# Attention heads of a fused four-layer kernel: more keys and values formed ahead, first expert rows fetched one stage earlier, deltas split in two parts

## The reference, cut to what matters

```
x = x + cross_attention0(layernorm(x), context)     # 16 heads of 16, softmax over 64 context rows
x = x + mixture0(layernorm(x))                      # 8 experts, top 2, then a layer norm of its own
x = x + cross_attention1(layernorm(x), context)
x = x + quantum_ffn(layernorm(x))
x = x + window_attention(context, layernorm(x))
x = x + mixture2(layernorm(x))                      # 8 experts, top 2, exact gelu
x = x + cross_attention3(layernorm(x), context)
x = x + ternary_ffn(layernorm(x))
```

## Time and profile before

| | us |
|---|---|
| median of three runs | 2132.32 |
| lowest and highest run | 2128.41 and 2132.96 |
| the profiled execution, its own time | 2133.32 |
| its span in the profile | 2131.5 |
| granted PE clock, mean | 0.945 of full |

### The profile page before, as it was taken

The page is one execution under the profiler, slowest core; times in us unless marked ns, Lnnn a source line. Parts: engine busy times, 40 slices in busy tenths (PEclk is TensorE's granted clock), DMA queues, the critical chain, the costliest instruction groups (busy, mean ns, idle before and its releaser), DMA issues. The chain is left out here.

```text
span 2131.5 us, 37545 instructions
## 1 busy us (share of the span) xinstructions
PE 1908.1 (90%) x11960; PEld 1414.1 (66%) x11961; DVE 1253.5 (59%) x2609; ACT 951.4 (45%) x2160; POOL 624.9 (29%) x716
## 2 busy tenths in 40 slices
PE   6999499999849996999999579999999995999787
PEld 3666356666526663666676379999999993666455
DVE  5787656666467876888655622222222214998886
ACT  2555434444346643333234333333333333555787
POOL 2223346656446721011001222222222222332000
PEclk9999699999969998999989589999999997999999
DMA  8000211121171004000001511111111114100001
GB/s 289 11 21 31 107 50 63 61 64 59 52 234 61 2 1 173 1 0 0 0 24 47 208 50 39 35 34 39 34 37 37 34 32 170 41 21 1 16 24 40
DMA packets 71619, 119.69 MB, mean 56 GB/s; under 512 B 13920, under 2 KB 55264, under 8 KB 68448
## 3 DMA queue, kind: packets, MB, share of 16 engines
q1 hardware_dynamic: 56304, 79.02, 10.6%
q0 software_dynamic: 13632, 37.24, 5.6%
q10 hardware_dynamic: 1584, 2.13, 0.3%
HBM read 87.03 MB, written 31.33 MB: 56 GB/s over the span
## 5 line engine op out<-in xcount | busy, mean ns | idle before, releaser
L1586 ACT ACTIVATE e_hT<-psum,x_bt 128x128 f32<-128x128 f32 x568 | 154.7, 383 | 340.4 <-PE psum L1549 340.4
L1549 PEld LDWEIGHTS psum<-e_xT,e_w 128*128 128x128 f32 x2272 | 266.4, 193 | 7.2 <-ACT e_xT L1579 3.6
L1549 PE MATMUL psum<-e_xT,e_w 128*128 128x128 f32 x2272 | 267.1, 276 | 3.0 <-ACT e_xT L1579 3.0
L1558 PE MATMUL psum<-m_w,e_hT 128*128 x1136 | 256.8, 379 | 0.0
L1558 PEld LDWEIGHTS psum<-m_w,e_hT 128*128 128x128 f32 x1136 | 210.4, 190 | 25.7
L1608 DVE COPY e_w<-m_w 128x2048 f32 x71 | 87.1, 1227 | 223.9 <-PE psum L1549 222.5
L1405 ACT ACTIVATE e_hT<-psum,x_bt,x_gt 128x128 f32<-128x128 f32 x284 | 107.0, 457 | 143.5 <-PE psum L1372 143.5
L1490 POOL DMA_INDIRECT rows_out<-e_y,dst x106 | 105.6, 996 | 207.0 <-DVE e_y L1618 175.1
L883 DVE TENSOR_REDUCE a_mx<-psum 128x16 f32<-128x1024 f32 x96 | 116.6, 1215 | 73.3 <-PE psum L631 73.1
L1482 POOL DMA_INDIRECT e_x<-rows_in,src x142 | 142.3, 1002 | 56.6 <-issue 35.3
L774 ACT ACTIVATE a_pT<-psum 128x512 f32<-128x512 f32 x192 | 103.9, 594 | 116.2 <-PE psum L687 116.1
(11 more groups left out here) (333 smaller groups left out, 3537.5 us busy)
## 6 DMA issues: line engine op xcount, KB each, us to landing
m_w<-in_L_ffn_w SPq DMA_DIRECT2D x16, 1024.0 KB, 12.1
m_w<-in_L_ffn_w SPq DMA_DIRECT2D x16, 512.0 KB, 11.1
m_w<-rows_out SPq DMA_DIRECT2D x16, 512.0 KB, 5.9
a_ar_g<-rows_out SPq DMA_DIRECT2D x16, 512.0 KB, 4.9
rows_in<-a_r_z SPq DMA_DIRECT2D x14, 512.0 KB, 2.9
x_res<-in_x SPq DMA_DIRECT2D x8, 512.0 KB, 7.4
m_w<-rows_in SPq DMA_DIRECT2D x8, 512.0 KB, 3.9
out_x<-x_res SPq DMA_DIRECT2D x8, 512.0 KB, 2.9
```

The source lines that it names most:

```text
L1549: mm = pe.matmul(h_b[s][:, f, :], w1[:, kk, f * P:(f + 1) * P], xT[s][:, kk, :], start=(kk == 0), stop=(kk == DC - 1))
L1558: mm = pe.matmul(y_b[s][:, 0:D], hT[s][:, f, :], k.w2[:, bass.ds(e * (FC * D) + f * D, D)], start=(f == 0), stop=(f == FC - 1))
L1586: g = act.activation(hT[s][:, f, :], h_b[s][:, f, :], ACT.Gelu, bias=bt[:, bass.ds(e * FC + f, 1)])
```

## The change

It has four parts. `held` is the number of batches whose keys and values are held at once, and `HEAD[L]` says how many of them PE forms at each of four places ahead of the loop.

1. **Keys and values ahead.** Layers 0 and 1 hold three batches: one is formed ahead of the turns, two after scores(0). Layer 3 holds all eight: four ahead of the turns, one after the turns, one after the queries, two after scores(0). Ahead of the loop they go into four banks that are otherwise unused there (`val_b`, `sum_b`, `out_b`, `pr_b`), one batch a bank in layers 0 and 1, two in layer 3, and are counted by a semaphore of their own, `kv_ps`. DVE drains a batch when all that shares its bank has been formed (`kv_formed`). In the loop step b forms batch b + held.
2. **Two banks for the first turns and queries.** For b = 0, c = 1 the turn and the queries use the bank `sc_b[1]`. Neither turn waits for a drain, and the queries wait for both turns' drains alone. On ACT `normalise(1)` moves behind the drains of the first queries (layers 0 and 3; in layer 1 it was there).
3. **First rows in the experts' stage.** SP itself waits for the scatters at the end of the stage, then issues the transfers of batch 0 (three in m0, two in m2), in `first_rows`. Their buffers, the experts' weights and the raw ternary weights are now parts of one tensor `m_wide`.
4. **Deltas in two parts.** `split_delta` runs for the 64 columns of batch 0 ahead of the first drain of keys, and for the other 448 where it stood.

The lines that carry it, cut:

```
+HEAD = {0: (1, 0, 0, 2), 1: (1, 0, 0, 2), 3: (4, 1, 1, 2)}
...
-        kb = [sb(f"{nm}kb{s}", [P, DC * GW]) for s in range(2)]
+        kb = [sb(f"{nm}kb{s}", [P, DC * GW]) for s in range(held)]
-        va = [sb(f"{nm}va{s}", [P, H // 2, 2, DK]) for s in range(2)]
+        va = [sb(f"{nm}va{s}", [P, H // 2, 2, DK]) for s in range(held)]
...
+        kv_banks = [val_b, sum_b, out_b, pr_b]
+        per = -(-held // len(kv_banks))
+        def kv_formed(b):
+            return min(held, (b // per + 1) * per) if b < held else b + 1
+        def front(b, c):
+            return sc_b[1] if b == 0 and c == 1 else pr_b
...
             def _(pool):
-                for s in range(2):
+                for s in range(held):
                     pool.memset(va[s][:, :, :, :], 0.0).then_inc(va_zero, 1)
...
                 def turn(b, c):
                     if c == 0:
                         pe.wait_ge(z_done, b + 1)
-                        pe.wait_ge(k_done, b + 1)
-                        pe.wait_ge(v_done, b + 1)
-                    else:
+                        if b:
+                            pe.wait_ge(k_done, min(NB, b - 1 + held))
+                            pe.wait_ge(v_done, min(NB, b - 1 + held))
+                    elif b:
                         pe.wait_ge(drained, DRAINS * b + 1)
...
                 def queries(b, c):
-                    pe.wait_ge(drained, DRAINS * b + 2 + c)
+                    pe.wait_ge(drained, DRAINS * b + 2 + (c if b else 0))
...
-                        if t == 3 and b + 2 < NB:
-                            keys_values(b + 2)
+                        if t == 3 and b + held < NB:
+                            keys_values(b + held)
...
-                keys_values(0)
+                after = [sum(formed[:i]) for i in range(len(formed) + 1)]
+                for b in range(after[0], after[1]):
+                    keys_values(b)
                 for c in range(DC):
                     turn(0, c)
+                for b in range(after[1], after[2]):
+                    keys_values(b)
                 for c in range(DC):
                     queries(0, c)
+                for b in range(after[2], after[3]):
+                    keys_values(b)
                 pe.wait_ge(drained, DRAINS)
                 pe.wait_ge(k_done, 1)
                 scores(0, 0, 0)
-                keys_values(1)
+                for b in range(after[3], after[4]):
+                    keys_values(b)
...
                 if loading:
-                    act.wait_ge(split, 7 + DSPLIT - 1)
+                    act.wait_ge(split, SPLITS)
...
-                drain_keys(0, 0)
-                drain_values(0, 0)
+                first = 3 if arrival else 1
+                if loading:
+                    split_delta(0, slice(0, S))
+                for b in range(first):
+                    drain_keys(b)
+                    drain_values(b)
...
                 if loading:
                     statistics(1)
-                    split_delta()
+                    split_delta(1, slice(S, NB * S))
                 if arrival:
                     arrival.add(dve, 1)
                     arrival.statistics(dve, 1)
+                early = held - formed[3]
+                for b in range(first, early):
+                    drain_keys(b)
+                    if b < held - 1:
+                        drain_values(b)
                 softmax(0, 0)
-                drain_keys(1, 1)
+                for b in range(early, held):
+                    drain_keys(b)
+                    if b < held - 1:
+                        drain_values(b)
...
             def _(sp):
                 if k.next_att is not None:
                     load_attention(sp, k, k.next_att)
+                    first_rows(sp, k, L)
...
+def first_rows(sp, k, L):
+    rows_sent(sp, k)
+    u, y = sum_buffers(k) if L == 0 else (None, got_buffers(k))
+    if L == 0:
+        sp.dma_start(u[0], normed_rows(k, 0)).then_inc(k.first_in[L], 16)
+    for j in range(TOPK):
+        sp.dma_start(y[j][0], expert_rows(k, j, 0)).then_inc(k.first_in[L], 16)
```

151 lines of the change are left out of this document (93 added, 58 removed).

## The result

| | before | after |
|---|---|---|
| median, us | 2131.02 (4 runs) | 2112.19 (4 runs) |
| lowest and highest | 2128.41, 2132.96 | 2107.66, 2114.22 |
| the profiled execution, its own time | 2133.32 | 2110.33 |
| its span | 2131.5 | 2108.5 |
| granted PE clock, mean | 0.945 | 0.948 |

The ratio is 0.9909, with a 95% interval of 0.9897 to 0.9921: 18.8 us less by the medians. The forecast was 2114.0, its range 2104 to 2124.

What follows compares the result with a forecast made beforehand. It took PE to bound the attention loops, with idle waits and low clock in the heads. Layers 0, 1 and 3 gave -7.6 - 4.7 - 7.0 = -19.3 us from 2133.3: forecast 2114, range 2104 to 2124.

Steps and rivals of the forecast that it cites:

- DVE is just in time: Layer 0's head: the second part of the split ends at 25.7, so the softmax starts at 26.7, not 32.97.
- rival (5): Softmax(0) held by the split's second part in layer 0, by drains 4 and 5 in layer 3; about 2130; chance 0.04.
- The barriers come 1.4 us later: End of m0 before layer 1: SP's 1.4 us of issue delays the barriers, to 589.4.
- they landed at 602.02 ... I take 599: Layer 1's head: batch 1's rows land at 599, between 597.3 and 602, so z comes 3.0 us earlier.
- low all through: Two banks for first turns and queries: worth 1.65 us a layer, with PE's clock low throughout.
- a case of -4.5 and one of -12.5: Layer 3: -4.5 if the four batches run at the low clock, -12.5 if it rises during them; -7 taken.
- 6.4 for both queries (the clock rising within them): Layer 3's head: both queries take 6.4 us, after 3.0 for the fifth batch; scores at 1795.7, 2.0 later than before.
- issue nothing: Costs put at nothing: `kv_ps` and the one tensor for weights and buffers add no instructions.
- (1): Layer 3's crowded head eats its gain; third context landing at 1779 makes it +1.5, total 2122.5; chance 0.13.
- (2): Clock rises in layer 3's four batches (-12.5) and layer 0's head is at its fast end (-9): 2107; chance 0.12.
- (3): The early fetch brings nothing: layer 1 becomes -0.5, layer 3 about -6, total 2119; chance 0.06.
- (4): Slower: clock stays at 1.2 GHz after PE's waits; decides at 45 us more low stretches, 2140 with 60; chance 0.03.

Runs made afterwards that it cites:

- the tensor alone: The kernel before, with only the experts' weights and raw ternary weights made parts of one tensor m_wide: 2127.39 us, ratio 0.9991.
- the first run: The changed kernel with batch 0's rows fetched in the attention stage again, not in the experts' stages: 2118.12 us, ratio 0.9936 to the kernel before.
- the contexts' experiment: The changed kernel, layer 3 issuing contexts of batches 0 to 3 before batch 1's rows, PE awaiting POOL's zeroes only before its scores: 2110.13 us, ratio 0.9898.
- the unused products: The changed kernel with 16 extra 128x512 products on PE in layer 1 ahead of the turns, their results unused: 2113.04 us, ratio 0.9904.

## Why the prediction was right

The median came out 1.8 us under the forecast, and the forecast's case held: the heads of all three attentions got shorter at the places named, and the loops by the batches that left them. Its terms were less good than its sum, and that the sum came so near is in part luck. By the two profiles the attentions gave 6.4 us more than forecast; 2.6 us that the rest took back, and 4.2 by which the two profiled executions lie further apart than the medians, made up for it. Undoing them one by one bears out parts 2, 3 and 4. For part 1 no run shows a gain that is clear of the spread: it shortens the loops, and the heads take all or much of it back.

**Layer 0**, -7.6 against -9.0 in the profile. Right: the turns start at 15.43 (forecast 15.25), nine passes over 64 columns took 2.3 us (2), the loop gives 1.6. The queries ran at the high clock, 3.70 us, where 6.3 were forecast, so the scores began at 22.66 and not at 25.3. Of these 2.6 us only 1.2 reached the softmax (25.54, forecast 26.7): "DVE is just in time" failed, since its second part of the split ended at 25.5 and the scores had been there since 23.9. This is rival (5) in small. From that softmax to the scores of tile 2 it took 7.7 us, forecast 7.9. The high clock of the queries was a matter of the execution: of the eight profiles with this code in layer 0 four have them at 3.70 us and four at 5.7 to 6.3, near the forecast, and the stage took 214.3 us on average in both groups. The mean is -8.2 against the profile before and -6.2 against that of the tensor alone; the term of -7.6 lies between.

**Layer 1**, -4.7 against -7.2. Three steps failed. "The barriers come 1.4 us later": they did not move. And "they landed at 602.02 ... I take 599": the rows of batch 1 were there 15.9 us after the last scatter, where 599 means 17.1. So z came 4.1 us earlier and not 3.0. From z to the first scores 3.3 us went instead of 1.65: the banks gave 1.5, and the clock, "low all through" in the forecast, rose within the queries (6.05 us, not 7.5). The third batch cost 1.6 behind the scores (1.5 forecast), and the loop gave 1.4 (1.6).

**Layer 3**, -7.0 against -9.5. The forecast had a case of -4.5 and one of -12.5, by the clock, and took a value between. The four batches did run at the low clock, as its slow case says, and held the turns, 3.2 us behind z. But then the clock rose: from the turns to the first scores it took 8.4 us, where the slow case has 13.6 (1782.1 to 1795.7). So the scores came 4.5 us earlier and not 2.0 later. The step that failed is "6.4 for both queries (the clock rising within them)", with the fifth batch at 3.0: they took 3.70 and 1.6. From the scores to those of tile 2 it was 3.4 us more than before (3.15 forecast), and the loop gave 8.4 and not 9.7: a batch whose keys and values leave this loop makes it 1.42 us shorter (22.36 to 20.94), where the term took the 1.62 that lie between their start and that of the next work. The same code gave 198.9, 199.0, 199.0, 200.3 and 202.6 us in five executions, that is -5.9 to -9.6. Between the ends of the forecast it is the clock that chooses, from one execution to the next.

**The rest.** The forecast put `kv_ps` and the one tensor at nothing because they "issue nothing". Still the tensor costs 2 us in m0's loop. Another 1.4 us of m0 went ahead of its first scatter (64.1 us from the stage's start, 62.7 before); with m_wide this took 62.1 to 65.2 from one profile to the next, so the 1.4 are not shown to come from the change.

**Rivals.** (1) needed the third context at 1779; PE went on without a pause from 1757.63. (2) came true in layer 0 alone, where the profile is at its fast end of -9: the four batches of layer 3 ran at the low clock. (3) fell with the first run. (4) fell too: by the mean granted clock the low stretches make up 2 x 0.055 x 2131.5 = 234 us before and 2 x 0.052 x 2108.5 = 219 after, shorter and not longer. Its mechanism exists in small, as the contexts' experiment shows: behind PE's waits of layer 3 the clock fell again and took back what the head had won. (5) shows in both layers (the first softmax is held until 25.54 and until 1778.24, for 1.6 and 2.1 us) but it doesn't decide.

The Trainium skill ("DMA: Bandwidth & Descriptors", Anatomy of one DMA) led to an estimate of 5.6 us for the three transfers, by which DVE would start its sum at once. The page gives that fit for transfers that GpSimd issues, and these are issued by SP. They were issued at 578.61 and DVE's wait ended at 585.75, 7.1 us later, much as before (6.95): the trace decides. Of DVE's 2.95 us of wait 1.5 are what the estimate missed, and 1.4 are there because the barriers did not move. That turns can't overtake the matmuls ahead of them ("TensorE: Matmul & The Clock Gate", The mechanism) agrees with layer 3, where they start at 1766.49 right behind the fourth batch, though z was done at 1763.3.

## What to carry to other kernels

Fetch what the next stage reads first in the stage that writes it: the 1.4 us of issue were hidden ahead of the barrier, and it freed the transfers queued behind it as well. Work that is moved from a loop bound by PE into its head can only pay where the head has idle time that it can reach, and here it was not shown to pay at all; ask which instruction ends the head, and count the drains on the other engine. Where PE pauses in a head, the clock decides over 3 to 4 us from one execution to the next, so judge such an edit by the shape of its waits, and by the total only over many runs. Take a second profile of the kernel before too: a gain is a difference of two executions, and here two executions of the attentions as they were before lay 4.5 us apart.

## What was not expected of the hardware

- The same instructions with the same pauses had the clock rise 14.6 us after PE's first product in one execution (1753.68 to 1768.3) and 20.9 us in another (1751.44 to 1772.3), with 3.6 us between the stages' lengths.
- In layer 1 PE had worked 7.3 us without a pause (588.6 to 595.9: 2.9 of keys and values, 4.4 of the unused products) when the clock rose to 2.4 GHz. With a pause of 13 us in that place it stayed at 1.2 until within the queries.
- A barrier between two stages took 6.04 us from the last scatter with and without 1.4 us of issue on SP, and 7.16 with 2.9.
- With the experts' weights inside one larger tensor, the loop of m0 took 1.8 to 2.6 us more, 0.025 to 0.037 us a tile, in thirteen profiles against one.
